# Two accumulation tables in place of four in the scatter stage of a graph network's first layer

## The chip, the cores and the metric

One core of a Trainium2 chip runs the whole program in one launch. The metric is the device time in microseconds, median of three runs. The profile is of one further execution of the same program.

## What the kernel computes

Four graph layers over 6250 nodes with 256 features and 100000 edges (sorted by destination), each followed by `x = layernorm(x + layer(x))`. The change touches the first layer alone:

```
gathered = edge_val[:, None] * x[edge_col]          # edge_row = src, edge_col = dst
support  = segment_sum(gathered, edge_row, N)       # summed by SOURCE node
out      = relu(concatenate([x, support], axis=1) @ W + b)
```

The second layer is an attention layer with two rounds, the third and fourth gather rows of a table by `src` and sum them by `dst`. They run after the first layer and are unchanged.

## The kernel before

The program is a sequence of stages with a barrier between them. The set-up loads the edges; then come the scatter stage (`scatter_by_source`), a short stage for degrees, the combination (`combine`), and then the other layers.

**Scatter stage.** The edges are cut into 784 tiles of 128. Since they are sorted by destination, the rows of `x` that a tile needs lie in one window of 128 rows. For each tile VectorE makes two 0/1 matrices (L973, L975), TensorE multiplies them (L918), ScalarE copies the product out of PSUM (L893), TensorE multiplies it with the window of `x` (L909), and ScalarE copies the 128 result rows to one of eight slots of `rows` (L884). GpSimd (POOL) then issues one indirect DMA that adds these 128 rows of 1 KB to rows of a table in HBM, chosen by an index (L845, `compute_op=ALU.add`). Within a tile, edges with the same source are summed first, and the repeats are sent to a spare block of rows, so that no row is named twice in a tile.

Two tiles in a row can name the same row, however, and two additions to it may not be in flight together. So there are `COPIES` tables, `support0` to `support3`; tile k goes to table `k % COPIES`, and POOL waits, before it issues tile k, until the DMA of tile k - COPIES has landed (L841 to L844 in the function below). Other waits of POOL are for the rows (`rows_ready`) and, once in eight tiles, for the index (`index_ready`).

Eight tiles are a half of the unrolled loop. Once in a half, SyncE loads the next window of `x` (L862, 128 KB) and the sources of eight tiles, broadcast to all partitions (L865, 512 KB). VectorE computes the index of the next half (L947 to L961), for which it waits until all scatters of the half before have landed; ScalarE waits, before it writes a slot of `rows`, for the landing of the scatter eight tiles back.

**Zeroing.** Before the first tile, VectorE fills `zeros` (L933) and POOL issues 16 DMAs of it (L829) that clear all tables. The scatter loop begins when they have landed.

**Combination.** It walks over 50 blocks of 128 nodes, in five iterations of ten, two halves of five blocks each. SyncE loads the block's rows from every table to `support_rows` (L1698); VectorE adds four copies to two (L1877, `two_sums`) and two to one (L1882, `support_sum`); TensorE transposes this (L1812) and multiplies (L1841); VectorE adds the bias (L1909), applies relu and the residual (L1935) and takes statistics (L1946). VectorE's program puts the additions for block j + 2 ahead of the use of block j's product.

Of the kernel before, what the change touches and what calls it, by code (L numbers as in the profile page):

```python
# [8 lines left out]
P = 128  # L9
# [4 lines left out]
ONEHOTS = 8  # L14
AHEAD = 16
WITHIN = 2
COPIES = 4
BIG = 1e30
WIDEST = 60.0

# [2 lines left out]
ALU = mybir.AluOpType  # L23
# [17 lines left out]
@contextmanager  # L41
def phase(nc, *names):

    sems = {n: nc.alloc_semaphore(name=f"{n}_{nc.next_id()}") for n in names}
    with nc.Block() as block:  # L45
        yield block, namedtuple("Semaphores", list(sems))(**sems)
    nc.clear_and_free_semaphores(list(sems.values()))

    nc.all_engine_barrier(sem_only=True)
# [12 lines left out]
def tiles_of(stack, nc):  # L62
    def sbuf(name, shape, dtype=FP32):
        return stack.enter_context(nc.sbuf_tensor(f"{name}_{nc.next_id()}", shape, dtype))

    def psum(name, shape=(P, 512), dtype=FP32):
        return stack.enter_context(nc.psum_tensor(f"{name}_{nc.next_id()}", list(shape), dtype))

    return sbuf, psum
# [714 lines left out]
def scatter_by_source(nc, g, support, spare, histogram, first_pass):  # L784
# [8 lines left out]
    with ExitStack() as stack:  # L793
        sbuf, psum = tiles_of(stack, nc)
        parts = 2 * HALF // COPIES
        zeros = sbuf("zeros", [P, (g.blocks + 1) * g.features // parts])
# [15 lines left out]
        with phase(nc, "zeroed", "x_loaded0", "x_loaded1", "row_loaded0", "row_loaded1", "own", "index_ready",  # L812
# [6 lines left out]
            def _(pool):  # L819

                pool.wait_ge(s.zeroed, 1)
                for slot in range(HALF):
                    for part in range(2):
                        if first_pass:
                            flat = support[slot % COPIES].rearrange("n f -> (n f)")
                            size = flat.shape[0] // parts
                            at = (2 * (slot // COPIES) + part) * size
                            target = flat[at:at + size].rearrange("(p z) -> p z", p=P)
# [5 lines left out]
                with pool.Fori(0, g.tiles // RING) as i:  # L834
                    for k in range(RING):
                        if k % HALF == 0:
                            pool.wait_ge(s.index_ready, i * 2 + (k // HALF + 1))
                        pool.wait_ge(s.rows_ready, i * RING + (k + 3))

                        before = (k - COPIES) % HALF  # L840
                        uses = (k - COPIES) // HALF + 1  # L841
                        pool.wait_ge(scattered[before], i * 32 + 16 * (uses + 2))

                        pool.sem_inc(s.issued, 1)  # L844
                        nc.gpsimd.indirect_dma_start(  # L845
                            support[k % COPIES],
                            bass.IndirectOffsetOnAxis(ap=index[:, k // HALF, k % HALF:k % HALF + 1], axis=0),
# [761 lines left out]
def steps(blocks):  # L1609

    return max(n for n in range(2, 12, 2) if blocks % n == 0)


def ring_of(body):


    depth = max(2, body // 2)
    return depth, min(2, depth - 1)


def combine(nc, g, spec):
# [17 lines left out]
    body = steps(g.blocks)  # L1639
    group = body // 2  # L1640
    depth, ahead = ring_of(body)

    def nodes(i, j, count=1):
        return bass.ds(i * (body * P) + j * P, count * P)
# [4 lines left out]
    with ExitStack() as stack:  # L1649
        sbuf, psum = tiles_of(stack, nc)  # L1650
        if both:
            support_rows = sbuf("support_rows", [P, 2, group, COPIES, spec.features])
            two_sums = sbuf("two_sums", [P, depth, 2, spec.features])
            support_sum = sbuf("support_sum", [P, depth, spec.features])
            x_rows = sbuf("x_rows", [P, depth, spec.features])
        if own_rows:
# [17 lines left out]
        def view(tile):  # L1674
            return tile[0:width, 0:chunks * P].rearrange("p (c n) -> p c n", c=chunks)

        def second_view(tile):
            return tile[0:width, chunks * P:2 * chunks * P].rearrange("p (c n) -> p c n", c=chunks)


        with phase(nc, "issued", "product_used", "added", "loaded0", "loaded1", "scaled", "copied", "turned", "summed", "left_ready",
                   "pairs_added", "selector_zeroed", "selector_ready", "own_added", "support_summed", "support_turned", "multiplied", "finished", "out_free",
                   "stored0", "stored1") as (block, s):
            loaded, stored = [s.loaded0, s.loaded1], [s.stored0, s.stored1]
            transfers = COPIES if both else 1
# [30 lines left out]
            def wait_loaded(engine, i, j):  # L1716
                if j % group == 0:
                    engine.wait_ge(loaded[j // group], i * (16 * transfers) + 16 * transfers)
# [137 lines left out]
            def _(dve):  # L1856
# [15 lines left out]
                def add_own(i, j):  # L1872
                    b = j % depth
                    if both:
                        wait_loaded(dve, i, j)
                        here = support_rows[:, j // group, j % group, :, :]
                        nc.vector.tensor_tensor(two_sums[:, b, :, :], here[:, 0:2, :], here[:, 2:4, :], ALU.add  # L1877
                                                ).then_inc(s.pairs_added, 1)
                        dve.wait_ge(s.pairs_added, i * body + (j + 1))

                        dve.wait_ge(s.multiplied, i * body + (j + 1))
                        nc.vector.tensor_tensor(support_sum[:, b, :], two_sums[:, b, 0, :], two_sums[:, b, 1, :],  # L1882
                                                ALU.add).then_inc(s.support_summed, 1)
                    elif turn:
                        dve.wait_ge(s.turned, i * body + (j + 1 + depth))

                        dve.wait_ge(s.left_ready, i * body + (j + 1))
                        if spec.heads:
                            nc.vector.tensor_tensor(unscaled[:, b, :, :], g.acc[0:width, 0:chunks, nodes(i, j)],
                                                    view(turned[b]), ALU.add).then_inc(s.own_added, 1)  # L1890
                            dve.wait_ge(s.own_added, i * body + (j + 1))
                            nc.vector.tensor_tensor(
                                sums[:, b, :, :], unscaled[:, b, :, :],
                                second_view(turned[b]),
                                ALU.mult).then_inc(s.summed, 1)
                        else:
                            nc.vector.tensor_tensor(sums[:, b, :, :], g.acc[0:width, 0:chunks, nodes(i, j)],
                                                    view(turned[b]), ALU.add).then_inc(s.summed, 1)
# [279 lines left out]
def build_program(nc, t, output):  # L2178
# [24 lines left out]
    with ExitStack() as stack:  # L2203
# [45 lines left out]
        with inner:  # L2249
            with ExitStack() as first:  # L2250
                histogram = tiles_of(first, nc)[0]("histogram", [3, padded])
                windows(nc, g, lambda first: scatter_by_source(nc, g, support, spare, histogram, first))
                degrees(nc, g, histogram)
            top, bottom = part("top", [P, 2, features]), part("bottom", [P, 2, features])
            bias = part("bias", [P, features])
            load(nc, (top[:], by_rows(t.L0_gnn_W[0:features, :])), (bottom[:], by_rows(t.L0_gnn_W[features:, :])),
                 (bias[:], on_all(t.L0_gnn_b)))
            combine(nc, g, spec(own="x", support=support, factor=[top, bottom], bias=bias, finish="relu"))
# [20 lines left out]
        with inner as held:  # L2279
            g.acc = part("acc", [P, 2, padded])  # L2280
            attend(nc, g, rows1, logits1, features, heads, segment[heads], scratch, planes)
            factor = part("factor", [P, 2, hidden + 2])
            attention_factor(nc, factor, t.L1_gnn_W2, t.L1_gnn_att_src2, t.L1_gnn_att_dst2, held)
            bias = part("bias", [P, 2])
            load(nc, *((bias[:, c:c + 1], t.L1_gnn_b1[c * P:(c + 1) * P].unsqueeze(1)) for c in range(2)))
            combine(nc, g, spec(own=rows1, heads=heads, factor=[factor], feature_bias=bias, rectify=True,
                                columns=hidden + 2, store=rows2, stored_columns=hidden + 1, finish="logits"))
# [4 lines left out]
        with inner:  # L2292
            g.acc = part("acc", [P, 2, padded])
            g.z = g.acc[0:1, 1, :]
            attend(nc, g, rows2, logits2, hidden, 1, segment[1], scratch, planes)
            factor = part("factor", [hidden, 1, features])
            feature_bias, bias = part("feature_bias", [hidden, 1]), part("bias", [P, features])
            load(nc, (factor[:], by_rows(t.L1_gnn_Wf)), (feature_bias[:], t.L1_gnn_b2.unsqueeze(1)),
                 (bias[:], on_all(t.L1_gnn_bf)))
            combine(nc, g, spec(own=rows2, features=hidden, heads=1, factor=[factor], feature_bias=feature_bias,  # L2300
                                bias=bias, finish="add"))
# [113 lines left out]
```

## Time and profile before

| | us |
|---|---|
| median of 3 runs (8930.01 to 8946.38) | 8934.65 |
| time of the profiled execution | 8930.71 |
| span of the profiled execution | 8926.4 |
| VectorE fills `zeros` to first scatter | 65.3 to 146.4 |
| scatters, first to last issue (784) | 146.4 to 1603.9 |
| combination, first load to last block | 1683.1 to about 1921 |

The span is the time from the first to the last instruction; 4.3 us lie outside it. All stages after the combination, some 7000 us, have no instruction that the change touches. An engine's idle time in a row of the timeline stands in brackets, with what ended it.

### The profile page before, as it was taken

What the parts mean: (1) busy time and instruction counts of PE and PEld (TensorE: products, weight loads), DVE (VectorE), ACT (ScalarE), POOL (GpSimd) and SP (SyncE); (2) the same over time, 40 slices, a digit from 0 to 9 for tenths busy, and PEclk for the clock granted to TensorE, in tenths of its full rate; (3) what the DMA queues carried; (4) which work ended last, traced back from release to release, by engine and by line L of the source; (5) the groups of instructions that cost most, each with busy time, mean ns of one, the idle gap of its engine ahead of it and who ended that gap; (6) DMA issues with size and microseconds to landing.
All of it is one profiled execution on the core that took longest, in us unless ns stands there. A gap on an engine that the chain in (4) does not pass through costs nothing. (4 is left out here: it accounts for less than half of the span.)

```text
span 8926.4 us, 128652 instructions
## 1 busy us (share of the span) xinstructions
PE 6316.5 (71%) x29880; PEld 4449.0 (50%) x29880; DVE 3522.3 (39%) x13590; ACT 1187.1 (13%) x4082; POOL 5927.0 (66%) x5622
## 2 busy tenths in 40 slices
PE   3777777562777867477776666667777777777777
PEld 1444444451444546122223665656665666656665
DVE  3444444343555553344446333322222222223333
ACT  1333333120000004000001111100000000000000
POOL 3888888104777750677751777757776777767776
PEclk9888888796898885666765888877877788777777
DMA  7777777321333321111111444434443444434443
GB/s 237 115 115 114 115 115 114 82 85 54 94 94 94 94 69 39 22 27 27 27 21 59 117 118 118 118 96 118 118 118 110 116 118 118 117 107 117 117 117 107
DMA packets 488461, 864.57 MB, mean 97 GB/s; under 512 B 110732, under 2 KB 332678, under 8 KB 485926
## 3 DMA queue, kind: packets, MB, share of 16 engines
q0 software_dynamic: 332512, 675.16, 33.1%
q1 hardware_dynamic: 155854, 188.39, 6.8%
q8 instruction: 30, 0.49, 0.0%
q14 instruction: 65, 0.53, 0.0%
HBM read 677.39 MB, written 185.75 MB: 97 GB/s over the span
## 5 line engine op out<-in xcount | busy, mean ns | idle before, releaser
L704 PE MATMUL bank<-onehots,rows 128*128 128x128 f32 x12544 | 2531.8, 350 | 941.9 <-DMA rows<-gcn_rows,index 569.2
L648 POOL DMA_INDIRECT rows<-gcn_rows,index x2352 | 2234.5, 950 | 815.7 <-issue 653.0
L704 PEld LDWEIGHTS bank<-onehots,rows 128*128 128x128 f32 x12544 | 2084.2, 242 | 1386.6 <-DMA rows<-gcn_rows,index 726.4
L115 POOL DMA_INDIRECT rows<-gat_rows,index x1568 | 1615.6, 1030 | 564.8 <-issue 459.8
L159 PE MATMUL sums<-onehots,scaled_rows 128*128 128x128 f32 (+1 forms) x4704 | 1089.8, 349 | 502.2 <-DVE scaled_rows L213 502.2
L845 POOL DMA_INDIRECT support<-rows,index x784 | 1218.3, 1554 | 310.1 <-DMA support<-rows,index 136.6
L159 PEld LDWEIGHTS sums<-onehots,scaled_rows 128*128 128x128 f32 (+1 forms) x4704 | 663.5, 202 | 1002.1 <-issue 686.5
L648 POOL DMA_INDIRECT rows<-norm,index x784 | 742.4, 947 | 469.2 <-ACT index L674 230.7
L735 DVE TENSOR_SCALAR onehots<-iota,half_offset,edge_values 128x128 f32<-128x128 f32 x3136 | 853.1, 359 | 168.7 <-issue 108.2
L162 PE MATMUL z_sums<-onehots,edge_weight 128*4 128x128 f32 (+1 forms) x3136 | 723.5, 320 | 0.0
L745 DVE TENSOR_TENSOR acc<-acc,bank 128x256 f32 x396 | 165.5, 418 | 1356.7 <-PE bank L704 1356.7
L918 PE MATMUL cross_bank<-same_source,onehots 128*128 128x128 f32 x1568 | 372.2, 325 | 445.4 <-DVE same_source L975 445.4
L909 PE MATMUL rows_bank<-x_window,cross 128*128 128x256 f32 x1568 | 612.7, 481 | 11.1 <-ACT cross L893 10.9
L918 PEld LDWEIGHTS cross_bank<-same_source,onehots 128*128 128x128 f32 x1568 | 342.6, 228 | 554.8 <-issue 336.7
L191 DVE TENSOR_TENSOR bound<-alpha,top 128x16 f32<-128x16 f32 (+1 forms) x392 | 66.9, 171 | 1045.2 <-DMA rows<-gat_rows,index 1045.2
L1361 POOL DMA_INDIRECT scratch<-a_dst,first_edge x100 | 97.2, 972 | 500.4 <-PEq L45 470.6
L973 DVE TENSOR_SCALAR onehots<-iota,half_offset 128x128 f32<-128x128 f32 x784 | 241.0, 307 | 360.8 <-PE counts_bank L924 278.8
L909 PEld LDWEIGHTS rows_bank<-x_window,cross 128*128 128x128 f32 x1568 | 264.7, 212 | 215.9 <-issue 192.2
L176 DVE TENSOR_SCALAR onehots<-iota,half_offset 128x128 f32<-128x128 f32 x1568 | 362.3, 299 | 14.6 <-PE z_sums L162 4.1
L669 ACT COPY index<-source 128x8 int32 (+1 forms) x392 | 77.4, 197 | 2158.0 <-DMA rows<-gcn_rows,index 1703.2
L884 ACT COPY rows<-rows_bank 128x256 f32<-128x256 f32 x784 | 291.7, 372 | 461.5 <-PE rows_bank L909 306.8
L131 ACT ACTIVATE edge_weight<-exponent 128x16 f32<-128x16 f32 (+1 forms) x392 | 82.6, 211 | 2007.1 <-DVE exponent L198 1996.3
(256 smaller groups left out, 5940.1 us busy)
## 6 DMA issues: line engine op xcount, KB each, us to landing
source_row<-in_src_flat SPq DMA_DIRECT2D x99, 512.0 KB, 4.7
rows<-gcn_rows,index POOLq DMA_INDIRECT x2352, 2.8
support<-zeros POOLq DMA_DIRECT2D x16, 1632.0 KB, 54.8
support_rows<-support SPq DMA_DIRECT2D x40, 640.0 KB, 7.3
rows<-gat_rows,index POOLq DMA_INDIRECT x1568, 2.7
gcn_rows<-out SPq DMA_DIRECT2D x150, 128.0 KB, 1.8
own_rows<-gcn_rows SPq DMA_DIRECT2D x150, 128.0 KB
x_window<-in_x SPq DMA_DIRECT2D x98, 128.0 KB, 2.7
```

The costliest lines, as they stand in the source:

```text
L115: nc.gpsimd.indirect_dma_start(rows[:, k, :], None, table, bass.IndirectOffsetOnAxis(ap=index[:, k:k + 1], axis=0),).then_inc(gathered[k], 16)
L159: last = nc.tensor.matmul(sums[h][c][0:width, 0:P], left[:, c * width:(c + 1) * width], onehots[:, k % ONEHOTS, :], start=first, stop=final)
L162: last = nc.tensor.matmul(z_sums[h][0:heads, 0:P], edge_weight[:, k // BATCH, k % BATCH, :], onehots[:, k % ONEHOTS, :], start=first, stop ...
L176: made = nc.vector.tensor_scalar(onehots[:, k % ONEHOTS, :], g.iota[:], g.half_offset[:, tile], None, ALU.is_equal)
L648: nc.gpsimd.indirect_dma_start(rows[:, k, :], None, table, bass.IndirectOffsetOnAxis(ap=index[:, k:k + 1], axis=0),).then_inc(gathered[k], 16)
L704: done = nc.tensor.matmul(by_chunk(banks[h])[:, c, :], rows[:, k, c * P:(c + 1) * P], onehots[:, k, :], start=first and c == 0, stop=final ...
L735: made = nc.vector.tensor_scalar(onehots[:, k, :], g.iota[:], g.half_offset[:, tile], weights[:, 0, tile], ALU.is_equal, ALU.mult)
L845: nc.gpsimd.indirect_dma_start(support[k % COPIES], bass.IndirectOffsetOnAxis(ap=index[:, k // HALF, k % HALF:k % HALF + 1], axis=0), rows ...
L884: nc.scalar.copy(rows[:, k % HALF, :], rows_bank[k % 2][:, 0:g.features]).then_inc(s.rows_ready, 1)
L909: nc.tensor.matmul(rows_bank[k % 2][:, 0:g.features], cross[:, k % BUFS, :], x_window[:, k // HALF, :], start=True, stop=True).then_inc(s. ...
L918: nc.tensor.matmul(cross_bank[k % 2][:, 0:P], onehots[:, b, :], same_source[:, b, :], start=True, stop=True)
L973: nc.vector.tensor_scalar(onehots[:, b, :], g.iota[:], g.half_offset[:, tile], None, ALU.is_equal)
```

## The change

`COPIES` becomes 2. With it go two of the four tables, the size of `zeros` (half as wide, since `parts` becomes 8; the number of zeroing DMAs stays 16), the distance of the wait of POOL (the landing of tile k - 2 in place of k - 4), the number of loads per half in the combination (two in place of four), and its first addition.

```diff
-COPIES = 4
+COPIES = 2
...
             support_rows = sbuf("support_rows", [P, 2, group, COPIES, spec.features])
-            two_sums = sbuf("two_sums", [P, depth, 2, spec.features])
...
                         here = support_rows[:, j // group, j % group, :, :]
-                        nc.vector.tensor_tensor(two_sums[:, b, :, :], here[:, 0:2, :], here[:, 2:4, :], ALU.add
-                                                ).then_inc(s.pairs_added, 1)
-                        dve.wait_ge(s.pairs_added, i * body + (j + 1))
-
                         dve.wait_ge(s.multiplied, i * body + (j + 1))
-                        nc.vector.tensor_tensor(support_sum[:, b, :], two_sums[:, b, 0, :], two_sums[:, b, 1, :],
+                        nc.vector.tensor_tensor(support_sum[:, b, :], here[:, 0, :], here[:, 1, :],
                                                 ALU.add).then_inc(s.support_summed, 1)
```

The semaphore `pairs_added` is removed too.

## Rows read from the trace of the kernel before

**Rows 1.** Windows: zeroing, scatter stage, combination; busy us by engine, granted clock, DMA share, GB/s

```profile
core 0: us, PE busy (x) PEld busy (x) DVE busy (x) ACT busy (x) POOL busy (x), PEclk, DMA share, GB/s
...
146.40:1605.50 1459.10, 1100.81 (x4690) 673.76 (x4688) 694.68 (x3417) 508.17 (x1661) 1218.26 (x784) 0.85 0.75 114
...
1683.00:1920.00 237.00, 153.18 (x798) 134.69 (x799) 103.99 (x244) 47.58 (x150) 0.00 (x0) 0.92 0.35 111
68.40:136.40 68.00, 0.00 (x0) 0.00 (x0) 5.39 (x1) 0.00 (x0) 8.61 (x16) 1.00 0.98 407
```

**Rows 2.** Source line L845, the scatter: durations in ns, and time from issue to landing

```profile
L845 POOL DMA_INDIRECT support<-rows,index x784: 1541/1542/1686, 146.4 to 1603.9; - x196
...
DMA to landing us min/median/max: 3.7/3.8/4.8
```

**Rows 3.** Waits in the scatter stage: us in total, times, longest

```profile
PE cross_bank L918 <- DVE same_source L975: 333.1, 97, 4.6
DVE index L961 <- DMA support<-rows,index: 315.1, 96, 4.2
...
POOL support L845 <- DMA support<-rows,index: 136.6, 442, 0.8
POOL support L845 <- issue: 91.1, 298, 0.4
```

**Rows 4.** Timeline of POOL: scatters; start us, us long, instruction, idle before it

```profile
146.40 1.66 POOL L845 DMA_INDIRECT support<-rows,index  x1 [69.37 <-ACT rows L884]
...
509.36 1.54 POOL L845 DMA_INDIRECT support<-rows,index  x1 [0.30 <-DMA support<-rows,index]
511.20 1.54 POOL L845 DMA_INDIRECT support<-rows,index  x1 [0.30 <-DMA support<-rows,index]
...
516.77 1.54 POOL L845 DMA_INDIRECT support<-rows,index  x1 [0.33 <-DMA support<-rows,index]
...
1603.91 1.54 POOL L845 DMA_INDIRECT support<-rows,index  x1 [0.30 <-issue]
```

**Rows 5.** Timeline of ScalarE: copies to slots of `rows`

```profile
145.02 0.37 ACT L884 COPY rows<-rows_bank 128x256 f32<-128x256 f32 x1 [0.96 <-PE rows_bank L909]
...
516.07 0.37 ACT L884 COPY rows<-rows_bank 128x256 f32<-128x256 f32 x1 [1.32 <-DMA support<-rows,index]
...
516.74 0.37 ACT L884 COPY rows<-rows_bank 128x256 f32<-128x256 f32 x1
```

**Rows 6.** Timeline of SyncE: the two loads of a half

```profile
509.26 0.34 SPq L862 DMA_DIRECT2D x_window<-in_x  x1
509.77 0.34 SPq L865 DMA_DIRECT2D source_row<-in_src_flat  x1
```

**Rows 7.** Timeline of the zeroing

```profile
65.33 2.78 DVE L933 MEMSET zeros<- 128x3264 f32 x1 [17.18 <-PEq L49]
...
68.42 8.61 POOL L829 DMA_DIRECT2D support<-zeros  x16 [67.15 <-DVE zeros L933]
...
136.47 0.35 DVE L947 SCALAR_TENSOR_TENSOR scrap<-source_row,source_float,earlier 128x128 f32<-128x128 int32 x1 [61.70 <-DMA support<-zeros]
```

**Rows 8.** Timeline of one block of the combination

```profile
1709.71 0.42 DVE L1909 TENSOR_TENSOR out<-product,bias 128x256 f32<-128x256 f32 x1 [2.53 <-PE product L1841]
...
1710.72 0.67 DVE L1877 TENSOR_TENSOR two_sums<-support_rows 128x512 f32<-128x512 f32 x1
1711.43 0.42 DVE L1882 TENSOR_TENSOR support_sum<-two_sums 128x256 f32<-128x256 f32 x1
...
1711.91 0.71 PE L1812 MATMUL turned<-identity,support_sum 128*128 128x128 f32 x4 [1.79 <-DVE support_sum L1882]
...
1714.39 0.42 DVE L1909 TENSOR_TENSOR out<-product,bias 128x256 f32<-128x256 f32 x1 [2.53 <-PE product L1841]
```

**Rows 9.** Combination: source line L1877, its first instance in the timeline, and the window before it

```profile
L1877 DVE TENSOR_TENSOR two_sums<-support_rows x50: 674/678/693, 1693.3 to 1913.5; 128x512 f32<-128x512 f32 x50
...
1693.31 0.69 DVE L1877 TENSOR_TENSOR two_sums<-support_rows 128x512 f32<-128x512 f32 x1 [16.13 <-DMA support_rows<-support]
...
1688.00:1690.00 2.00, 0.00 (x0) 0.00 (x0) 0.00 (x0) 0.00 (x0) 0.00 (x0) 0.50 1.10 350
```

More of the change, by code:

```diff
@@ L1681, in combine @@
         with phase(nc, "issued", "product_used", "added", "loaded0", "loaded1", "scaled", "copied", "turned", "summed", "left_ready",
-                   "pairs_added", "selector_zeroed", "selector_ready", "own_added", "support_summed", "support_turned", "multiplied", "finished", "out_free",
+                   "selector_zeroed", "selector_ready", "own_added", "support_summed", "support_turned", "multiplied", "finished", "out_free",
                    "stored0", "stored1") as (block, s):
```

## The prediction

> **What bounds the kernel now.** The whole program is a chain of stages, so I read by stage. The windows [rows 1] give three that the change touches: the zeroing (68 us, DMA share 0.98), the scatter stage (1459 us) and the combination (237 us). Everything after that, some 7000 us, keeps its instructions. In the zeroing the DMA engines are the bound. In the scatter stage the busiest engine by time is POOL, 1218 of 1459 us, against 1101 for TensorE and a DMA share of 0.75.
>
> The source view of the scatter line and the list of waits say how POOL is bound. One scatter holds POOL for 1.54 us [rows 2], and between two scatters 0.30 us pass that are put down to "DMA" or "issue" alike [rows 3, 4]. The label "DMA" means little: 136.6 us over 442 times is 0.31 us each, as long as with no wait at all (91.1 / 298 = 0.31). So a scatter starts every 1.54 + 0.30 = 1.85 us, back to back, and the wait for the landing four tiles back is nearly free: four periods are 7.4 us, and a scatter lands 3.8 us after its start [rows 2]. From first to last start the 783 periods take 1603.91 - 146.40 = 1457.5 us, 1.861 each [rows 4]. TensorE, ScalarE and VectorE run ahead and wait for landings, VectorE alone 315 us [rows 3].
>
> In the combination one block's cycle is serial: VectorE adds, TensorE transposes and multiplies, VectorE uses the product, and each idles for the other (2.53 us and 1.79 us) [rows 8]. The cycle is 1714.39 - 1709.71 = 4.68 us.
>
> **What goes.** *Zeroing.* From the first issue at 68.42 to VectorE's start at 136.47 [rows 7] 68 us pass, for 16 DMAs of 1632 KB (26.7 MB), at a full DMA share; some 3 us of them are the start before the data flow. Half the bytes take (68 - 3) / 2 = 32 us less. The issues (8.6 us) and the fill of `histogram` (5.4 us) fit under the 35 us that are left. The fill of `zeros` halves: 2.78 / 2 = 1.4 us. Sum: -33 us. Bounds: -30 if the smaller transfers run less well, -34 at most.
>
> *Combination.* The removed addition stands in the serial cycle: from its start to that of the next one 1711.43 - 1710.72 = 0.71 us [rows 8], and TensorE waits right behind. The remaining addition keeps its shape (128 x 256) and its 0.42 us. 50 blocks [rows 9] by 0.71 = 35.5 us. The first block waits for four loads of 640 KB, until 1693.31, at 350 GB/s [rows 9]; two loads less are 1.31 MB, 3.7 us. Sum: -39 us. Below nothing it can't be, as nothing is added here; the smallest gain would be 30 us, if something else of the cycle filled a part of the 0.71.
>
> **What comes.** Now POOL may start tile k only when tile k - 2 has landed. Two periods are 3.69 us, and a landing alone takes 3.8. What counts is landing plus the time that POOL needs from the landing to its next start. The trace has one place where both are seen. The scatter that starts at 509.36 is the one that the scatter at 516.77 (four later) waits for, and it is also the one that ScalarE's copy of 516.07 waits for (eight later, same slot) [rows 4, 5]. ScalarE starts 516.07 after the same landing; POOL starts 0.70 us behind it, with an idle time just above its usual. ScalarE itself needs some time from the landing, which I take as 0.08. So POOL needs about 0.78 us from landing to start. The very first scatter points the same way: ScalarE's copy ends at 145.02 + 0.37 = 145.39 and POOL starts at 146.40, 1.01 us later [rows 4, 5]. Bounds: 0.07 (if a queue that always waits loses no more than ScalarE does) and 1.01; I take 0.78, since it is measured on this very wait. Behind the wait on POOL stands only the next scatter. The cover that this wait had is gone: the 0.30 us between scatters used to run beside it.
>
> A pair of scatters then takes 3.8 + 0.78 = 4.58 us, 2.29 each: 783 x 2.29 = 1793 us.
>
> *The bursts.* Once in a half (98 times) SyncE loads 640 KB [rows 6]. The scatter that starts with it at 509.36 lands only just before 516.07, about 6.6 us after its start, 2.8 over the usual; the next, 511.20, releases ScalarE's copy at 516.74, 5.5 us after its start, 1.7 over [rows 4 to 6]. With four tables this hid in the slack of 7.4 us. With two it is on the path, but once and not summed over both scatters, since they run side by side in two chains that only hold their order. I expect 2.2 us a half; at least 0.8, if most bursts fall between scatters that are now further apart, at most 3.2, if the order of the two chains adds to it. 98 x 2.2 = 216 us (78 to 314).
>
> The stage then takes 1793 + 216 = 2009 us, from first to last start, in place of 1457.5: +551 us.
>
> *What feeds POOL.* TensorE needs 1101 / 98 = 11.2 us a half at a granted clock of 0.85 [rows 1]; a half now lasts 8 x 2.29 + 2.2 = 20.5 us in place of 14.9, so it and the index (which waits for a landing of the half before) have more room than now.
>
> *A rule on the landing.* The scatter moves 128 KB and lands 3.8 us after its start [rows 2]. The Trainium skill, "DMA: Bandwidth & Descriptors", section "Anatomy of one DMA — SWDGE (gpsimd) path", fits a DMA of the gpsimd path as 2.0 us plus bytes over 436 GB/s; that is 2.3 us here, an estimate by that page. By it the wait two back would be free, which is the first rival below. The trace disagrees if 2.3 is counted from the start, and agrees if it is counted from the end of the 1.54 us on POOL (1.54 + 2.3 = 3.84).
>
> **The sum.** -33 - 39 + 551 = +479 us. On the profiled execution's own time, 8930.7, this gives 9410 us. Its time lies 4 us below the median, which is nothing beside the bounds.
>
> **The rivals.**
>
> 1. *The wait two back stays free, so the kernel gets faster.* With two chains in place of four the scatters might land earlier, so that landing and start-up fit under 3.69 us. Then POOL stays at 1.85 and only the savings count: -72 us, 8859 us. It decides from a period of 1.861 + 72 / 783 = 1.953 us on, that is 3.9 us for landing and start-up together, bursts included. Against it: the least landing in the stage is 3.7 [rows 2], which leaves 0.2 for a start-up of 0.78. Chance 0.04.
>
> 2. *The start-up is not paid.* If POOL restarts as fast as ScalarE, the pair takes 3.8 + 0.07 = 3.87, 1.94 each: 783 x 1.94 = 1519, with the bursts 1735, +277 - 72 = +205: 9136 us. For it: the labels of the waits cannot tell it, and I have few places. Against it: the 0.70 us of [rows 4, 5]. Chance 0.07.
>
> 3. *The bursts stay hidden*, as the DMA engines have more gaps: 1793 us, +335 - 72 = +263, 9194 us. Against it: source loads start about when a landing releases ScalarE and TensorE, which is when a new scatter starts. Chance 0.09.
>
> 4. *The feed becomes the bound.* If TensorE, with longer pauses, were granted 0.5 throughout, its work would take 11.2 x 0.85 / 0.5 = 19 us a half, plus some 3 us in which it waits for VectorE after the index (333.1 / 97 = 3.4) [rows 3]: 22.4 x 98 = 2195, +738 - 72 = +666, 9597 us. Chance 0.06.
>
> The forecast has the rest, 0.74. Its own range has 0.8 to 3.2 us a half and pairs of 4.5 to 4.65 us. Low end: 783 x 2.25 = 1762, + 78 = 1840, +383 - 72 = +311, 9242 us. High end: 783 x 2.325 = 1820, + 314 = 2134, +677 - 72 = +605, 9536 us. These leave out more than 2 in 10, so the range reaches on to rival 3: 9190 to 9535 us, with 0.83 in it; rivals 1, 2 and 4 stay outside, 0.17.
>
> By a change of 0.2% (18 us), about what this kernel's measurement can tell from none: faster 0.04 (rival 1), the same 0.01 (between rivals 1 and 2), slower 0.95.
>
> **What would show it.** The scatters' starts 2.3 us apart in the quiet part of a half, in pairs' rhythm of 4.6 us, POOL idle 0.7 to 0.8 us before each with "DMA" as the releaser nearly every time; its 1.54 us unchanged; a longer step once a half; landing still 3.8. The scatter stage near 2010 us. VectorE's first index at about 103 us in place of 136.5. The combination's cycle 3.97 us. It would be wrong if the landing moves with the number in flight, or if POOL's start-up behind a real wait is not 0.78 us; both act on all 783 periods, 0.1 us of a pair being 39 us.

## The result and the profile after

The changed kernel takes 9372.95 us (median of 4 runs, 9364.7 to 9383.12), the one before 8933.05 us: 1.0491 times as long, 95% interval 1.0478 to 1.0504, 440 us more. The prediction said 9410 us, in a range of 9190 to 9535. The profiled execution took 9383.1 us, 10 us over the median, with a span of 9378.6, 452 us over the span of before; the stages below are read from it.

First the windows of the changed kernel: scatter stage, zeroing, combination, and all that follows. The rows answer to [rows 1].

```profile
115.40:2099.40 1984.00, 1179.11 (x4690) 706.80 (x4688) 686.44 (x3417) 496.92 (x1661) 1213.61 (x784) 0.75 0.56 84
66.40:105.40 39.00, 0.00 (x0) 0.00 (x0) 5.39 (x1) 0.00 (x0) 8.58 (x16) 1.00 0.94 377
...
2173.00:2371.00 198.00, 145.61 (x800) 127.20 (x800) 70.11 (x196) 47.25 (x150) 0.00 (x0) 0.95 0.22 70
...
2371.00:9378.60 7007.60, 5019.53 (x24170) 3600.48 (x24170) 2664.78 (x9835) 616.32 (x2253) 4697.84 (x4816) 0.76 0.32 89
```

POOL works as long as before (1214 against 1218 us), but in 1984 us; the DMA share falls from 0.75 to 0.56 and TensorE's granted clock from 0.85 to 0.75. No engine and no DMA engine is full: the stage is bound by a wait. The tail keeps its 7000 us.

Next, the source view of the scatter line and the waits from 110 to 2050 us, nearly the whole stage, as in [rows 2, 3].

```profile
L845 POOL DMA_INDIRECT support<-rows,index x784: 1541/1541/1696, 115.4 to 2097.8; - x196
...
DMA to landing us min/median/max: 3.6/3.8/7.2
```

```profile
DVE index L961 <- DMA support<-rows,index: 765.6, 95, 11.5
...
POOL support L845 <- issue: 304.8, 394, 40.4
POOL support L845 <- ACT rows L884: 297.6, 293, 4.2
...
POOL support L845 <- DMA support<-rows,index: 191.6, 76, 4.6
```

The scatter itself still takes 1.54 us and still lands after 3.8. The 783 steps take 2097.8 - 115.4 = 1982.4 us, 2.53 each. The trace holds the landing of only 392 of the 784 scatters (196 in the kernel before), so the longest one can be longer than this view says. The labels of POOL's idle time stay of little use: of 794 us only 192 are put down to the DMA, 298 to ScalarE, 305 to nothing (40 of these 305 are one wait, before the first scatter). The time of the starts tells what the labels don't. This is POOL's timeline of the changed kernel, and SyncE's, for the same stretch:

```profile
519.56 1.54 POOL L845 DMA_INDIRECT support<-rows,index  x1 [0.30 <-issue]
522.35 1.54 POOL L845 DMA_INDIRECT support<-rows,index  x1 [1.25 <-issue]
524.19 1.54 POOL L845 DMA_INDIRECT support<-rows,index  x1 [0.30 <-ACT rows L884]
526.90 1.54 POOL L845 DMA_INDIRECT support<-rows,index  x1 [1.16 <-issue]
528.74 1.62 POOL L845 DMA_INDIRECT support<-rows,index  x1 [0.30 <-issue]
531.38 1.54 POOL L845 DMA_INDIRECT support<-rows,index  x1 [1.02 <-ACT rows L884]
533.38 1.54 POOL L845 DMA_INDIRECT support<-rows,index  x1 [0.46 <-ACT rows L884]
537.79 1.54 POOL L845 DMA_INDIRECT support<-rows,index  x1 [2.86 <-DMA support<-rows,index]
```

```profile
530.66 0.34 SPq L862 DMA_DIRECT2D x_window<-in_x  x1
531.18 0.35 SPq L865 DMA_DIRECT2D source_row<-in_src_flat  x1
```

From 522.35 to 526.90 is 4.55 us, from 524.19 to 528.74 also 4.55: a pair takes 3.8 + 0.78. Within a pair the second scatter follows 1.85 us behind the first, as soon as POOL is free, and then POOL waits. At 531.18 the half's loads start; the scatter of 531.38 lands late, and the one two behind it starts at 537.79, 6.4 us later in place of 4.55. That is a burst on the path. How much such bursts cost in all can be added up from POOL's starts: each start is set against the start two scatters back, and what goes beyond 4.55 us is counted, halved since there are two chains. That gives 201 us in the stage, and 188 of them fall on the four scatters behind each half's loads, 14 on the others.

Last, the two parts that got shorter. The first fence is the zeroing, as in [rows 7], the second the combination, as in [rows 8, 9]; VectorE's lines have moved up, L1877 is the one addition that is left and L1904 uses the product.

```profile
64.63 1.42 DVE L933 MEMSET zeros<- 128x1632 f32 x1 [16.81 <-PEq L49]
...
66.37 8.62 POOL L829 DMA_DIRECT2D support<-zeros  x16 [65.09 <-DVE zeros L933]
...
105.42 0.35 DVE L947 SCALAR_TENSOR_TENSOR scrap<-source_row,source_float,earlier 128x128 f32<-128x128 int32 x1 [32.71 <-DMA support<-zeros]
```

```profile
2183.73 1.10 DVE L1877 TENSOR_TENSOR support_sum<-support_rows 128x256 f32<-128x256 f32 x3 [12.72 <-DMA support_rows<-support]
...
2360.03 0.41 DVE L1877 TENSOR_TENSOR support_sum<-support_rows 128x256 f32<-128x256 f32 x1
2360.49 0.71 PE L1811 MATMUL turned<-identity,support_sum 128*128 128x128 f32 x4 [1.06 <-DVE support_sum L1877]
...
2362.97 0.42 DVE L1904 TENSOR_TENSOR out<-product,bias 128x256 f32<-128x256 f32 x1 [2.53 <-PE product L1840]
...
2363.98 0.41 DVE L1877 TENSOR_TENSOR support_sum<-support_rows 128x256 f32<-128x256 f32 x1
```

The first scatter starts at 115.4 in place of 146.4, 31 us sooner. The cycle of a block is 2363.98 - 2360.03 = 3.95 us in place of 4.68, with VectorE's wait of 2.53 us unchanged: the removed addition was on the path. The combination as a whole, from its first load to its last statistics, went from 239 to 195 us, 44 less. The account: -31 + 525 (1982.4 - 1457.5) - 44 = +450, of 452 us in the spans.

### The profile page after: what moved, and what is told of

Same layout as the page of the kernel before. It is cut to its first block and busy times, and to the rows that moved or that the text cites. A ratio compares the mean times of both kernels' runs of the same rounds, so it can differ in the third digit from the quotient of the medians.

```text
span 9378.6 us, 128517 instructions
## 1 busy us (share of the span) xinstructions
PE 6393.8 (68%) x29880; PEld 4480.9 (48%) x29880; DVE 3475.3 (37%) x13540; ACT 1175.5 (13%) x4082; POOL 5920.6 (63%) x5622
## 5 line engine op out<-in xcount | busy, mean ns | idle before, releaser
L845 POOL DMA_INDIRECT support<-rows,index x784 | 1213.7, 1548 | 810.7 <-issue 315.2
L918 PE MATMUL cross_bank<-same_source,onehots 128*128 128x128 f32 x1568 | 399.5, 345 | 751.6 <-DVE same_source L975 751.6
L918 PEld LDWEIGHTS cross_bank<-same_source,onehots 128*128 128x128 f32 x1568 | 365.1, 244 | 870.9 <-issue 484.5
L909 PE MATMUL rows_bank<-x_window,cross 128*128 128x256 f32 x1568 | 649.4, 501 | 115.7 <-ACT cross L893 115.3
L924 PE MATMUL counts_bank<-onehots,values 128*3 128x128 f32 x1568 | 355.1, 316 | 0.0
```

Of the source, the lines that this page charges most:

```text
L845: nc.gpsimd.indirect_dma_start(support[k % COPIES], bass.IndirectOffsetOnAxis(ap=index[:, k // HALF, k % HALF:k % HALF + 1], axis=0), rows ...
L909: nc.tensor.matmul(rows_bank[k % 2][:, 0:g.features], cross[:, k % BUFS, :], x_window[:, k // HALF, :], start=True, stop=True).then_inc(s. ...
L918: nc.tensor.matmul(cross_bank[k % 2][:, 0:P], onehots[:, b, :], same_source[:, b, :], start=True, stop=True)
L924: nc.tensor.matmul(counts_bank[k // HALF][0:3, 0:P], values[:, k // HALF, k % HALF, :], onehots[:, b, :], start=(k % HALF == 0), stop=(k % ...
```

## The experiments

When e5 to e8 were run, the kernel before took 10320 us, since its later layers were slower there; why is not known. The scatter stage, which e8 leaves as it was, was not slower (1459.5 us, from 146.5 to 1606.0), so these four are read by stage or against the kernel before of the same session. e2, e3, e6, e7 and e9 are one execution each.

**e1, four tables, wait two back.** In the kernel before:

```diff
-                        before = (k - COPIES) % HALF
-                        uses = (k - COPIES) // HALF + 1
+                        before = (k - 2) % HALF
+                        uses = (k - 2) // HALF + 1
```

> Four tables as before, but POOL waits for the landing two tiles back. Theory (landing plus start-up, two chains): the stage from first to last scatter takes as long as with two tables, 1982 us, since the number of tables only matters through the wait; the kernel takes the time before plus 525 us, about 9458. The pair's step is the landing of 3.8 us plus 0.78. Rival (fewer tables are slower by themselves, as rows of one table are hit more densely): the stage is shorter than 1982 us by what the tables cost, down to 1458.

Measured: 9452.8 us against 8943.6, 1.0568 (1.0551 to 1.0586), 509 us more. The source view of its scatter line:

```profile
L845 POOL DMA_INDIRECT support<-rows,index x784: 1541/1542/1706, 144.9 to 2114.5; - x196
...
DMA to landing us min/median/max: 3.5/3.8/7.4
```

The stage takes 1969.6 us, 13 less than with two tables. So 512 of the 525 us come from the distance of the wait alone; 13 us, 0.7% of the stage, are left for the tables themselves, and one execution of each is not enough to say that they are real.

**e2, wait three back**, the same edit with 3.

> Four tables, POOL waits for the landing three tiles back. Theory: a quiet triple has 3 x 1.85 = 5.5 us of room for 4.6 us of landing and start-up, so it stays at 1.85 us a scatter; only the scatters that land late beside a half's loads (5.5 to 6.7 us) stop POOL. With the landings of the kernel before put in one by one, the stage takes 1576 us, 118 more than before: about 9050 us. Rival (any shorter distance costs in proportion): a third of the step between four and two, or half of it, 170 to 260 us more.

Measured: 9039.7 us, 96 more than before; the stage from 146.1 to 1710.1, 1564 us, 106 more. As the theory had it: most steps are 1.85 us, and only late landings stop POOL.

**e3, wait one back**, the same edit with 1.

> Four tables, POOL waits for the landing of the tile just before: one chain, in which each late landing counts in full. Theory: every step is landing plus 0.78 us, 4.6 in the quiet, and 783 x 4.58 = 3586 us plus up to 98 x 3.5 us for the late landings, 3590 to 3930 us for the stage; POOL's idle time is 3.0 us before each scatter. Kernel about 11060 to 11410 us. Rival (a start-up of under 0.2 us when the queue has nothing else to do): 783 x 4.0 = 3130 us.

Measured: 11114 us; the stage from 145.6 to 3786.6, 3641 us, 4.65 a step. Its timeline of POOL:

```profile
1007.09 1.54 POOL L845 DMA_INDIRECT support<-rows,index  x1 [3.02 <-DMA support<-rows,index]
1011.62 1.66 POOL L845 DMA_INDIRECT support<-rows,index  x1 [2.99 <-ACT rows L884]
1016.29 1.54 POOL L845 DMA_INDIRECT support<-rows,index  x1 [3.00 <-ACT rows L884]
...
1038.89 1.54 POOL L845 DMA_INDIRECT support<-rows,index  x1 [2.96 <-DVE index L961]
```

With one chain, 3.0 us of idle plus 1.54 is the whole of landing and start-up: 4.54 us, the 3.8 + 0.78 of the prediction less the rounding. A start-up under 0.2 us would show 2.5 us of idle at most. The label names three different releasers for the same wait.

**e4, the savings alone.** The changed kernel, but its scatters go to four tables with the wait four back:

```diff
 COPIES = 2
+TABLES = 4
...
-                        before = (k - COPIES) % HALF
-                        uses = (k - COPIES) // HALF + 1
+                        before = (k - TABLES) % HALF
+                        uses = (k - TABLES) // HALF + 1
...
-                            support[k % COPIES],
+                            support[k % TABLES],
```

> The scatters go to four tables with the wait four back, as before, but only two tables are zeroed and only two are read and added in the combination (the sum leaves out half of the tiles). This is all that the change removes, without its wait. Forecast of the prediction: 72 us less than before, 8861 us. From the trace of the changed kernel: 31 us less to the first scatter and about 42 less in the combination, 73 to 76 in all.

Measured: 8865.5 us against 8943.6, 0.9914 (0.9898 to 0.9931), 78 us less. The stage took 1461 us (113.9 to 1575.2). So what the change removes is worth 78 us, and e1 and e4 together (+509 - 78 = +431) give the 440 of the change but for 9 us, less than the intervals of the two leave open.

**e5 and e9, the sources loaded twice**, to a buffer `twice` that nobody reads, in the changed kernel (e5) and in the kernel before (e9):

```diff
+                        sync.wait_ge([s.again0, s.again1][h], i * 16 + 16)
+                        sync.dma_start(
+                            twice[:, h, :, :].rearrange("p k e -> p (k e)"),
+                            g.source_flat[0:1, bass.ds((i * 2 + h) * (HALF * P), HALF * P)]
+                            .to_broadcast([P, HALF * P])).then_inc([s.again0, s.again1][h], 16)
```

> The changed kernel, and SyncE loads the sources of each half a second time to a buffer that nobody reads: 512 KB more a half, at 350 GB/s 1.5 us of the DMA engines. Theory (late landings are on the path, once per half): the stage's excess over 783 x 2.29 us, now 183 us or 1.9 a half, grows by up to 1.5 us a half, 147 us; between 60 and 150 us more. Rival (the step is fixed by landing and start-up alone, or by the feed from TensorE): no change.

Measured: the stage from 117.7 to 2188.9, 2071 us, 89 more than with two tables, within the theory's 60 to 150.

> The kernel before, four tables and the wait four back, with the sources of each half loaded twice, as in the run with two tables. Theory: four steps give 7.4 us of room, of which landing and start-up take 4.6; the landings get later (up to about 7 or 8 us), so a few stop POOL: the stage takes 1460 to 1500 us, 0 to 40 more than before, where two tables lost 89. Rival (the loads take bandwidth from the scatters whatever the distance): 89 us more here too.

Measured: 9030.4 us against 8932.2; the stage from 147.6 to 1703.0, 1555 us, 98 more than before. My theory failed here, and its rival's 89 is near. The longest landing seen reached 8.9 us. The four steps of 7.4 us leave 6.6 us for a landing when the start-up of 0.78 is taken off, so POOL did stop, which it hardly does before; it didn't wait for rows, which from the ninth scatter on were ready at least 4.4 us ahead of its start:

```profile
331.04 1.54 POOL L846 DMA_INDIRECT support<-rows,index  x1 [0.30 <-issue]
335.36 1.54 POOL L846 DMA_INDIRECT support<-rows,index  x1 [2.78 <-DMA support<-rows,index]
```

So e5 and e9 don't tell the theories apart: four tables hide the loads of the kernel before, but not those with the sources loaded twice. What sets how late a scatter lands beside them was not tried.

**e6, all rows to the spare block**, the changed kernel with `repeats > -1` in place of `repeats > 0.5`, so that each scatter names the same 128 rows in a row.

> The changed kernel, but every row is added to the spare block, so that each scatter goes to the same 128 rows of its table, one after another in memory (the output lacks the sums). It is the base for the next run, and tells whether the landing depends on which rows are hit. Theory: landing 3.8 us and the stage near 1982 us, within 40. Rival (scattered rows are what makes the landing long): a landing clearly under 3.8 us and a shorter stage.

Measured: the stage from 115.1 to 2051.0, 1936 us, 46 less than with the real rows, just past the 40 that I allowed. So which rows are hit matters little, at most 46 us. Whether the landing itself is still 3.8 us can't be read, as this trace has no time from issue to landing.

**e7, the same with small loads**, 32 KB of `x` and 64 KB of sources a half in place of 640 KB (both buffers are filled once ahead of the loop):

```diff
-                        sync.dma_start(x_window[:, h, :], g.x_dram[bass.ds(base, P), :]).then_inc(x_loaded[h], 16)
+                        sync.dma_start(x_window[:, h, 0:64], g.x_dram[bass.ds(base, P), 0:64]).then_inc(x_loaded[h], 16)
...
-                            source_row[:, h, :, :].rearrange("p k e -> p (k e)"),
-                            g.source_flat[0:1, bass.ds((i * 2 + h) * (HALF * P), HALF * P)]
-                            .to_broadcast([P, HALF * P])).then_inc(row_loaded[h], 16)
+                            source_row[:, h, 0, :],
+                            g.source_flat[0:1, bass.ds((i * 2 + h) * (HALF * P), P)]
+                            .to_broadcast([P, P])).then_inc(row_loaded[h], 16)
```

> As the run before, and each half loads 64 KB of sources and 32 KB of x in place of 640 KB (stale rest, the output lacks the sums). Theory: without late landings the step is landing plus 0.78 over two, 2.29 us, and the stage takes 1793 us, some 190 less than the run before. Rival (the excess comes from the order of the chains or the feed): it stays within 50 us of the run before.

Measured, the source views of e6 and of e7:

```profile
L845 POOL DMA_INDIRECT support<-rows,index x784: 1542/1542/1699, 115.1 to 2051.0; - x196
```

```profile
L845 POOL DMA_INDIRECT support<-rows,index x784: 1541/1541/1681, 115.4 to 1954.3; - x196
```

The stage takes 1839 us, 97 less, half of the 190 that I expected (143 counted from e6), and still 46 over the 783 x 2.29 = 1793 us of quiet pairs. So the big loads cost about 97 us in this setting, 1.0 us a half. Neither theory nor rival fits: the rival allowed 50. Where the rest is, the starts tell, added up as for the changed kernel: in e6 the excess over pairs of 4.55 us is 155 us, in e7 58 us, and in both all of it falls on the four scatters behind a half's loads, small as these are in e7; the other scatters have none. So the rest isn't lost by two chains holding each other up all along. Nor is it the feed: the rows of a scatter were ready at least 9 us ahead of its start in both (all but the first eight). In e7 nearly all of the 58 us, 46, stand behind one of the two halves' loads of the loop of sixteen tiles. Why a landing beside those is still late is open.

**e8 and e10, the sum one block further ahead**, in the kernel before. In the combination VectorE and TensorE wait for each other in each block; the edit moves the addition from block j + 2 to block j + 3:

```diff
-                    for j in range(ahead):
+                    lead = ahead + 1 if both else ahead
+                    for j in range(lead):
                         add_own(i, j)

                     for j in range(body + 2):
-                        if j + ahead < body:
-                            add_own(i, j + ahead)
+                        if j + lead < body:
+                            add_own(i, j + lead)
```

> The kernel before, four tables and the wait four back, with one edit in the combination: VectorE adds the copies of block j + 3 ahead of the use of block j, in place of j + 2. Theory: in the combination VectorE and TensorE wait for each other in one cycle of 4.68 us; with the sum made a block earlier TensorE's 1.79 us of waiting goes, and the cycle comes to TensorE's own 2.9 us or a little more, 3.0 to 3.5: 45 to 70 us less, 8863 to 8888 us. Rival (ScalarE's copies or the product's buffer hold the cycle): no more than 15 us less.

Measured: 10265.5 us against 10319.8 in that session, 0.9940 (0.9922 to 0.9957), 54 us less.

> The kernel before with VectorE's sum one block further ahead, once more and with more rounds: in the earlier run the combination was over 56 us sooner after its start than before, and the kernel 54 us faster. The same 50 to 60 us here, a ratio of about 0.994, clear of 0.2%.

Measured: 8873.5 us against 8932.2, 0.9934 (0.9920 to 0.9948), 59 us less. The timeline of e10's combination:

```profile
1711.44 0.42 DVE L1909 TENSOR_TENSOR out<-product,bias 128x256 f32<-128x256 f32 x1 [0.48 <-PE product L1841]
...
1712.45 0.67 DVE L1877 TENSOR_TENSOR two_sums<-support_rows 128x512 f32<-128x512 f32 x1
...
1713.16 0.43 DVE L1882 TENSOR_TENSOR support_sum<-two_sums 128x256 f32<-128x256 f32 x1
...
1714.06 0.42 DVE L1909 TENSOR_TENSOR out<-product,bias 128x256 f32<-128x256 f32 x1 [0.48 <-PE product L1841]
```

The cycle is 2.62 us with both additions in it, against 4.68 before and 3.95 with one addition removed. That is less than the 3.0 to 3.5 us that I expected, and by itself it would save 50 x 2.06 = 103 us. It doesn't, since only seven of the nine steps inside an iteration of ten blocks take this long (the last two take 1.73 us, with and without the edit), and the step from one iteration to the next grows (it was between 10.0 and 11.8 us, and is between 12.5 and 12.8): there VectorE makes one more sum ahead and waits 3.1 to 3.4 us for its loads. So my 45 to 70 us came out in part by luck, a better cycle against a longer start. This version keeps the four tables and is faster than both kernels.

## Why the prediction was right

- **Zeroing, -33 us: measured -31.** The zeroing itself went from 68.1 to 39.1 us (66.37 to 105.42), 29 less in place of 32: over the zeroing the DMA engines moved 377 GB/s against 407 [rows 1]. The fill of `zeros` gave its 1.4 us, and the set-up ended a little sooner.
- **Combination, -39 us: measured -44.** 50 x (4.68 - 3.95) = 37 and the first loads, 2183.73 - 2177.22 = 6.5 us in place of 10.2, 3.7 less. The other 4 us lie at the four later starts of an iteration, where VectorE had waited about 1 us for its loads and now doesn't; I had left these out. The addition stands in only seven of the ten steps of an iteration, five of them of 4.68 us; the other three additions come ahead of its first product. They were not hidden there either (the first step from one iteration to the next fell from 10.1 to 7.1 us), so 50 x 0.71 came out, though I had read it off the cycle alone. e4 has both savings without the wait: 78 us in place of my 72.
- **The start-up of 0.78 us.** The one place in the trace of before carried the forecast, and it held: pairs of 4.55 us with two chains, steps of 4.54 with one (e3). It is no matter of one place any more: in the changed kernel POOL stood for more than 0.35 us before 326 scatters whose awaited landing is in the trace, and 314 of them started 0.775 to 0.803 us behind that landing, the other 12 1.4 to 2.1 us. Rival 2, which would not pay it, is out. The median landing stayed at 3.8 us with one, two, three or four in flight (e3, changed kernel and e1, e2, before), so rival 1, the faster kernel, had nothing to stand on. Counted from the scatter's start, the formula of the Trainium skill ("DMA: Bandwidth & Descriptors", section "Anatomy of one DMA — SWDGE (gpsimd) path") gives 2.3 us, an estimate by that page, and the trace does not agree; counted from the end of the 1.54 us on POOL it gives 3.84, and the trace, with 3.8, does.
- **The bursts, +216 us: measured about 190.** 1982.4 - 1793 = 189 us, 1.9 us a half in place of 2.2. This is the term that was mis-sized, by 27 us, as much as 9410 lies above the profiled execution; the 10 us that are missing to 37 lie between that execution and the median. (The zeroing's 2 us too much and the combination's 5 us too little are small and of opposite sign.) That the excess stands beside the loads holds: 188 of the 201 us over pairs of 4.55 us fall on the four scatters behind them. Of these, e7 shows 97 us for the size of the loads; the rest it leaves open. Rival 3, hidden bursts, is out, since the scatter of 531.38 shows one on the path.
- **The feed.** TensorE's granted clock fell, as rival 4 needs, but to 0.75 and not to 0.5; its work is 1179 / 98 = 12 us in halves of 20, and POOL's starts follow landings. After the first eight scatters the rows of a scatter were ready at least 9 us ahead of its start, and the index of each half at least 7 us. Rival 4 is out.
- **The tables themselves** cost nothing that can be told (e1).
- **Two of the signs did not come as written.** POOL's idle time is not 0.7 to 0.8 us before each scatter but about 0.3 and 1.2 in turn, since the second of a pair follows the first at once; only their sum is what I had. And the DMA is named as the releaser 77 times in 784, not nearly every time.

## What to carry to other kernels

The number of copies of a target is here the number of DMAs in flight. Work out what they cover: (landing + start-up of the queue) / (time of one on the queue), here 4.6 / 1.85 = 2.5, so two are too few and three just fail beside other transfers; below this number the stage goes by latency, though each engine gets idler. Read the price of a wait that does not bind yet from the rare places where it does, by the distance between the landing and the next start on the queue, since the label of idle time named three releasers for one wait. And before copies are removed to save an addition, see whether the addition has to stand in the cycle at all: making the sum one block earlier gave 59 us here, with all four copies kept.

## What the hardware showed beside this

From a landing to POOL's next indirect DMA pass 0.78 us, while ScalarE reacts 0.70 us sooner to the same landing [rows 4, 5]; where POOL is not stopped, only 0.30 us stand between two scatters. A scatter that adds 128 rows of 1 KB to a table lands 3.8 us (median) after its start with one, two, three or four in flight, but beside 640 KB of loads up to 7.2 us (changed kernel) or 7.6 us (e4), and with 1152 KB a half up to 8.9 us (e9). When all scatters name the same 128 rows, the stage is only 46 us shorter (e6).
